# Other units for the value projections, late value chunks, and side blocks of a fused differential attention and gated layer

## The reference, cut to what matters

```
xn = layernorm(x)
q1, k1, q2, k2 (each 16 heads x 8), v (16 heads x 16) = split(xn @ Wqkv)
A_b = causal softmax(q_b k_b^T / sqrt(8)) @ v          for b = 1, 2
d = A1 - lam * A2;  d = d / rms(d) * (1 - LAMBDA_INIT)
ffn = (gelu(xn @ Wg0) * (xn @ Wg1)) @ Wlinear           in fp8
out = x + d @ Wproj + ffn
```

## Time and profile before

| | |
|---|---|
| median of three executions | 184.43 us |
| the profiled execution | 184.12 us |
| its span | 182.3 us |
| PE busy | 175.5 us, 96% |
| ACT busy | 163.2 us, 90% |
| DVE busy | 92.4 us, 51% |
| POOL busy | 63.5 us, 35% |
| exponentials (L497) | 97 instructions, 138.1 us |
| products with values (L1062) | 776 instructions, 78.1 us |
| scores (L1050) | 384 instructions, 48.3 us |

### The profile page before, as it was taken

The page is one execution under the profiler, slowest core; times in us unless marked ns, Lnnn a source line. Parts: engine busy times, 40 slices in busy tenths (PEclk is TensorE's granted clock), DMA queues, the critical chain, the costliest instruction groups (busy, mean ns, idle before and its releaser), DMA issues.

```text
span 182.3 us, 4305 instructions
## 1 busy us (share of the span) xinstructions
PE 175.5 (96%) x1816; PEld 76.3 (42%) x1816; DVE 92.4 (51%) x219; ACT 163.2 (90%) x146; POOL 63.5 (35%) x81
## 2 busy tenths in 40 slices
PE   6999999999999999999999999999999999989992
PEld 6785344543332333343234434334524434432481
DVE  1878789312233230640374121706542789979982
ACT  3586678999999999999999999999999999999820
POOL 8449920052017322360622063217303560323000
PEclk9999999999999999999999999999999999999999
DMA  5996888780000000000277875000000000000015
GB/s 152 382 333 227 219 197 201 175 189 19 0 0 5 0 0 4 0 4 0 42 204 179 210 173 127 0 0 4 4 0 0 4 0 4 0 0 4 0 58 180
DMA packets 8935, 15.02 MB, mean 82 GB/s; under 512 B 2000, under 2 KB 5584, under 8 KB 8912
## 3 DMA queue, kind: packets, MB, share of 16 engines
q1 hardware_dynamic: 8080, 13.92, 28.0%
q10 hardware_dynamic: 832, 0.79, 1.3%
HBM read 5.26 MB, written 1.05 MB: 35 GB/s over the span
## 4 chain that ended last, share of the span: by engine, by line
PE 82%; DVE 11%; ACT 2%; DMA 2%; issue 1%; DVEq 0%
PE ps L1062 35%; PE ps L1050 20%; PE ps L904 12%; PE ps L970 7%; PE ps L1098 4%; DVE o_t L719 2%; PE ps L914 2%; DMA x_sb<-L_attn_x 2%; DVE parts L625 1%; PE ps L894 1%; PE ps L1103 1%; DVE parts L737 1%; ACT L455 1%; DVE area L630 1%; DVE xn_t L763 1%
## 5 line engine op out<-in xcount | busy, mean ns | idle before, releaser
L497 ACT ACTIVATE probs<-ps,shift 128x1536 f32<-128x1536 f32 (+1 forms) x97 | 138.1, 1582 | 0.2 <-PE ps L1050 0.2
L1062 PE MATMUL ps<-probs,v_all 128*32 128x512 f32 (+3 forms) x776 | 78.1, 492 | 1.0 <-DVE o_t L719 0.8
L393 POOL TENSOR_SCALAR_AFFINE_SELECT probs<-probs 128x1024 f32<-128x1024 f32 (+1 forms) x40 | 36.7, 918 | 94.9 <-ACT probs L497 94.8
L1050 PE MATMUL ps<-q_st,k_st 32*128 32x512 f32 (+3 forms) x384 | 48.3, 411 | 0.0
L1050 PEld LDWEIGHTS ps<-q_st,k_st 32*128 32x128 f32 x384 | 22.5, 182 | 61.5 <-ACT probs L497 43.4
L719 DVE STREAM_TRANSPOSE o_t<-ps 128x512 f32<-128x512 f32 x16 | 11.5, 717 | 45.0 <-PE ps L1062 45.0
L1062 PEld LDWEIGHTS ps<-probs,v_all 128*32 128x32 f32 x776 | 16.4, 108 | 18.7 <-issue 9.7
L970 PE MATMUL ps<-area 128*128 128x512 fp8e4 x64 | 14.4, 379 | 0.2 <-DVE parts L625 0.2
L473 ACT ACTIVATE probs<-ps 128x512 bf16<-128x512 f32 x16 | 9.6, 597 | 3.7 <-PE ps L970 3.1
L644 DVE TENSOR_TENSOR area<-ps,probs 128x512 fp8e4<-128x512 f32 x16 | 10.9, 685 | 1.9 <-ACT probs L473 1.7
L970 PEld LDWEIGHTS ps<-area 128*128 128x128 fp8e4 x64 | 6.0, 98 | 8.0 <-issue 0.8
(11 more groups left out here) (90 smaller groups left out, 126.5 us busy)
## 6 DMA issues: line engine op xcount, KB each, us to landing
q_st<-parts SPq DMA_DIRECT2D x32, 128.0 KB, 2.8
k_st<-parts SPq DMA_DIRECT2D x32, 128.0 KB, 2.8
probs<-L_ffn_w_gating SPq DMA_DIRECT2D x4, 512.0 KB, 7.6
probs<-L_ffn_w_linear SPq DMA_DIRECT2D x1, 1024.0 KB, 12.4
out<-probs SPq DMA_DIRECT2D x3, 256.0 KB, 2.3
x_sb<-L_attn_x ACTq DMA_DIRECT2D x2, 256.0 KB, 5.1
w_q<-L_attn_Wqkv SPq DMA_DIRECT2D x1, 512.0 KB, 9.4
w_q<-L_attn_Wqkv SPq DMA_DIRECT2D x1, 256.0 KB, 4.2
```

Source lines behind the costliest of these rows:

```text
L393: pool.affine_select(out=blocks, in_=blocks, pattern=pattern, compare_op=ALU.is_ge, fill=0.0, base=0, channel_multiplier=-1).then_inc(mask ...
L497: act.activation(probs[:, at:at + PER_UNIT, cols], ps[:, 3 * (n % 2):3 * (n % 2) + 3, cols], ACT.Exp, bias=shift[:, br, 1, hg * BR + br:hg ...
L1050: ins = pe.matmul(ps[:, bank, at:at + wide * P], k_st[rows, g % STACKS, kb * P:(kb + 1) * P], q_st[rows, g % STACKS, queries], start=True, ...
L1062: ins = pe.matmul(ps[32 * j:32 * j + 32, 6, q0 % HALF:q0 % HALF + wide * P], v_all[:, g % HG, kb, 32 * j:32 * j + 32], probs[:, slot + j, ...
```

## The change

Value blocks 2 to 6 are projected one unit later (from unit 0 on one block a unit), and block 7 in two halves in units 8 and 9. Value chunks 3 to 8 of groups 0 to 3 are multiplied six units behind their scores in place of five, those of group 4 six behind for chunks 3 to 5 and five behind for 6 to 8 (before: five, and four); group 5 keeps its four behind for chunks 3 to 5 and its three for the last ones. The queries and keys of branch 2 stand in units 10 to 38 in place of 8 to 37. The blocks of the gated layer's last product, two squares, the residual additions, the first residual rows and the first output projection move. On DVE the copy of the last value block goes behind the first take, `keep(2, 0)` ahead of `split(6)`, and the `down` calls later. In the ending, residual 6 goes to the front.

```
-V_AT = {0: (1, 2), 1: (3,), 2: (4,), 3: (5,), 4: (6,), 5: (7,)}
-QK_AT = {8: (4, 0, 0, 256), 9: (4, 0, 256, 256), 13: (4, 1, 0, 512), 17: (5, 0, 0, 512), 20: (5, 1, 0, 256),
-         21: (5, 1, 256, 256), 25: (6, 0, 0, 512), 29: (6, 1, 0, 512), 32: (7, 0, 0, 256), 33: (7, 0, 256, 256),
-         37: (7, 1, 0, 512)}
+V_AT = {0: (1,), 1: (2,), 2: (3,), 3: (4,), 4: (5,), 5: (6,)}
+LAST_V_AT = (8, 9)
+QK_AT = {10: (4, 0, 0, 512), 14: (4, 1, 0, 512), 20: (5, 0, 0, 256), 21: (5, 0, 256, 256), 22: (5, 1, 0, 512),
+         26: (6, 0, 0, 512), 32: (6, 1, 0, 256), 33: (6, 1, 256, 256), 34: (7, 0, 0, 512), 38: (7, 1, 0, 512)}
 NORM_AT = 41
-DOWN_AT = {44: (0, 0, 4), 45: (0, 4, 8), 49: (1, 0, 8), 53: (2, 0, 8), 56: (3, 0, 4), 57: (3, 4, 8), 64: (4, 0, 8),
-           67: (5, 0, 4), 68: (5, 4, 8), 75: (6, 0, 8), 78: (7, 0, 4), 79: (7, 4, 8)}
-REST_AT, Y_AT = 83, 87
+DOWN_AT = {45: (0, 0, 4), 46: (0, 4, 8), 50: (1, 0, 8), 56: (2, 0, 4), 57: (2, 4, 8), 58: (3, 0, 8), 67: (4, 0, 4),
+           68: (4, 4, 8), 75: (5, 0, 8), 78: (6, 0, 4), 79: (6, 4, 8), 83: (7, 0, 8)}
+REST_AT, Y_AT = 87, (90, 91)
...
 def due(g, c):
-    late = ((5, 5), (5, 5), (5, 5), (5, 5), (5, 4), (4, 3), (3, 3), (3, 2))[g][c >= 6]
+    late = ((5, 6, 6), (5, 6, 6), (5, 6, 6), (5, 6, 6), (5, 6, 5), (4, 4, 3), (3, 3, 3), (3, 3, 2))[g][c // 3]
...
-                    if (g, c) in ((1, 2), (1, 5), (2, 5), (3, 0)):
+                    if (g, c) in ((1, 2), (2, 0), (2, 5), (3, 0)):
-                    if (g, c) in ((4, 4), (5, 2), (6, 0), (6, 5)):
+                    if (g, c) in ((4, 5), (5, 4), (6, 5), (7, 2)):
...
-            for b in range(0, TB, 2):
+            for b in range(0, TB - 2, 2):
                 values_in(b)
+            values_in(TB - 2, (0,))
...
-            keep(0, 0)
+            take(0, 0)
+            values_in(TB - 2, (1,))
+            divide(0, 0)
...
+            keep(2, 0)
             split(6)
-            keep(2, 0)
             split(7)
             keep(2, 1)
...
+                keep(3, 1)
                 down(0)
-                keep(3, 1)
...
+                if n in LAST_V_AT:
+                    if n == LAST_V_AT[0]:
+                        pe.wait_ge(v_out, TB - 1)
+                    project_values(TB - 1, LAST_V_AT.index(n))
...
+                elif g == 0 and c == 5:
+                    pe.wait_ge(v_out, TB)
...
-                    if n == Y_AT:
+                    if n in Y_AT:
                         pe.wait_ge(wp_in, 16 * 8)
                         pe.wait_ge(out_t_ready, 2)
-                        project(0, 0)
-                        project(1, 0)
+                        project(Y_AT.index(n), 0)
...
             def ending():
                 values_due(UNITS, 0, GROUPS)
                 values_due(UNITS + 1, 0, GROUPS)
+                pe.wait_ge(res_ready, TB // 2)
+                residual(6, start=True)
                 pe.wait_ge(out_t_ready, 3)
...
-                project(6, 0, start=True)
-                pe.wait_ge(res_ready, TB // 2)
-                residual(6)
+                project(6, 0)
```

More of the change, by code:

```diff
@@ L403, in _ @@
                     mask(g, c)
-                    if (g, c) in ((1, 2), (1, 5), (2, 5), (3, 0)):
-                        square_of(4 + ((1, 2), (1, 5), (2, 5), (3, 0)).index((g, c)))
-                    if (g, c) in ((4, 4), (5, 2), (6, 0), (6, 5)):
-                        residual(((4, 4), (5, 2), (6, 0), (6, 5)).index((g, c)))
+                    if (g, c) in ((1, 2), (2, 0), (2, 5), (3, 0)):
+                        square_of(4 + ((1, 2), (2, 0), (2, 5), (3, 0)).index((g, c)))
+                    if (g, c) in ((4, 5), (5, 4), (6, 5), (7, 2)):
+                        residual(((4, 5), (5, 4), (6, 5), (7, 2)).index((g, c)))
         @block.scalar
@@ L770, in turn_back, with values_in @@
                               ).then_inc(out_t_ready, 1)
-            def values_in(b):
-                dve.wait_ge(v_ready, b // 2 + 1)
-                for e in range(2):
+            def values_in(b, blocks=(0, 1)):
+                dve.wait_ge(v_ready, b // 2 + 1 + (b == TB - 2 and blocks == (1,)))
+                for e in blocks:
                     dve.tensor_copy(v_all[:, :, b + e, :].rearrange("p g (j w) -> p g j w", j=J)[:, :, :, 0:DV],
@@ L830, in _ @@
             with dve.If(large2 == 0):
+                keep(3, 1)
                 down(0)
-                keep(3, 1)
             all_of, first, last = slice(0, 32), slice(0, 16), slice(16, 32)
             take(4, 0)
-            down(1)
             own.step(difference(0, 0))
@@ L839, in _ @@
             take(4, 1)
+            down(1)
             own.step(difference(0, 1))
@@ L842, in _ @@
             take(5, 0)
-            down(2)
             own.step(difference(1, 0))
@@ L846, in _ @@
             take(5, 1)
+            down(2)
             differ(1, 1)
@@ L850, in _ @@
             mean_of(1, 1)
-            down(3)
             inverse_root(slice(0, 64))
@@ L858, in _ @@
             mean_of(2, 0)
+            down(3)
             take(6, 1)
@@ L916, in queries_keys, with project_values @@
                                  skip_group_check=True)
-            def project_values(b):
+            def project_values(b, only=None):
                 if b == 0:
                     pe.wait_ge(wv_in, 16)
-                for k in range(KC):
+                for k in range(KC) if only is None else (only,):
                     ins = by_quarters(V_BANK[b // 2], b % 2 * C, xn_t[:, k, b * P:(b + 1) * P], w_q[:, k, 2 * C:3 * C],
                                       k == 0, k == KC - 1)
-                if b % 2 == 1:
+                if (b % 2 == 1 or b == TB - 2) and only != 0:
                     ins.then_inc(v_ready, 1)
@@ L1092, in second_half @@
                 pe.wait_ge(o_taken, 2 * g + 1)
+                if g == 0:
+                    pe.wait_ge(v_out, kb + 1)
                 product(g, MIXED, first[1] * P, kb, wide, q0, True)
```

## The result

Seven executions of the changed kernel took 189.5 to 193.43 us, median 190.09; the kernel before beside them 184.31. The ratio is 1.029, interval 1.0276 to 1.0305. The forecast was 188.5 in a range of 187.1 to 189.4: the direction and most of the mechanism held, the range did not. In three of the seven (192.48 to 193.43) TensorE's clock was granted at half for some microseconds in the attention, in the other four (189.5 to 190.09) hardly or not at all, and the ratio is made of those four. The lowest of the four already lies over the range. In a second set of six it was 189.14 to 193.24. Both profiled executions of this kernel are among those with the lower clock.

The account below looks back on a forecast made before the run. PE and ACT, both near full, bound the kernel. ACT's losses of 5.7 less 1.46 before give +4.25; with +0.28 and -0.35, +4.2 on 184.12 is 188.3, by the median 188.5, range 187.1 to 189.4.

Parts of the forecast that it names:

- Bound by both engines, lost time adds up: Whole attention: PE 96% and ACT 90% busy; PE's waits are lost for ACT too, except for at most 0.7 us slack.
- Value block out of unit 0: Units 0 and 1: one block instead of two between scores 0 and 1; exponential 1 at 34.32, a gain of 0.32.
- Borders: Next group's first chunk waits for DVE's take: stall 0.47 at units 18, 30, 54 and 65, 0.15 at 42.
- Query block at 34: Unit 34: query block's first pass waits until DVE has emptied bank 7; stall 1.24, with scores 35 queued behind.
- Bound and collision at 45: Unit 45: v(3,2)'s second half waits behind branch 2's bound, stall 1.2 for 0.4; POOL's mask holding L567 adds 0.7.
- Rival A: Unit 45: the small L567 slips past POOL's mask, so time is 0.7 less, 187.8; chance 0.28.
- Units 90 and 91: Output projection's first pass moves into these half-empty units; their slack is gone and ACT loses 0.13 there.
- Ending: Residual 6 runs ahead of the wait for DVE on PE's last stretch: gain 0.35 (0 to 0.43).
- The +0.28 for the later last product: End of attention: ACT trails the last scores by 0.56 instead of 0.85, so the last product comes 0.28 later.
- Rival C: Four borders: waits shorter by half, 4 x 0.25 less; 187.5 with the collision, 187.0 without; chance 0.08.
- rival D: Late values cost PE 0.86 instead of 1.00 per unit, slack swallows every 0.47; 183.6 by the median; chance 0.02.
- rival B: More POOL collisions, at (7,2)'s mask and D7's cast: two more PE waits of 0.4 to 0.7, 189.4; chance 0.10.

Follow-up runs that it names:

- The last experiment: Changed kernel with the two halves of the first DOWN block back in units 44 and 45, filling part of PE's wait: median 189.24 us, ratio 1.0256.
- the kernel with the take first: Changed kernel with the take of v(3,2)'s first half ahead of the last part of branch 2's bound on DVE: median 188.67 us, ratio 1.0216.

## Why the prediction was right and wrong

ACT's losses, forecast and measured as the distance of the starts of its exponentials less 1.4227 us a unit. The last experiment stands for the changed kernel with the clock full, but for unit 55, where the kernel with the take first shows 0.15. The kernel before loses 1.45.

| units | forecast | clock full (part of the wait filled) | changed kernel, lower clock |
|---|---|---|---|
| 1 to 18 | 0 | 0.00 | 0.01 |
| 19 | 0.39 | 0.47 | 0.46 |
| 20 to 30 | 0.21 | 0.23 | 0.20 |
| 31 | 0.48 | 0.57 | 0.56 |
| 32 to 34 | 0.15 | 0.13 | 0.15 |
| 35 | 1.25 | 1.25 | 1.25 |
| 36 to 45 | 0.55 | 0.66 | 0.65 |
| 46 | 0.69 + 0.7 | 1.38 | 1.97 |
| 47 to 54 | 0 | 0.02 | 2.04 |
| 55 | 0.09 | 0.00 | 0.56 |
| 56 to 65 | 0.20 | 0.13 | 0.14 |
| 66 | 0.49 | 0.64 | 0.64 |
| 67 to 95 | 0.63 | 0.91 | 0.92 |
| sum | 5.83 | 6.38 | 9.57 |

*Bound by both engines, lost time adds up:* right. With the wait at unit 34, the one at 45 and the borders gone, 9.6 or 6.4 go back to 1.67.

*Value block out of unit 0:* right; exponential 1 is on ACT's own pace and units 1 to 18 lose nothing (0.59 before).

*Borders:* right in place and kind, small in size. At units 19, 31 and 66 ACT loses 0.47, 0.57 and 0.64 where 0.39, 0.48 and 0.49 were forecast. The next group's chunk starts 1.99 to 2.00 after the last one where 1.90 was reckoned. The prediction took the 0.77 from a take's start to PE from a half chunk's, and a half chunk's it is again in the changed kernel (101.23 to 102.00), but a whole chunk starts 0.86 after its take's start. At unit 65 it is 2.07, since the take too starts later behind its chunk (1.21 for 1.13). The four borders and unit 42 together: some 0.4.

*Query block at 34:* right to 0.01, shown by undoing it.

*Bound and collision at 45:* right, 1.38 for 1.39 in the kernel that stands in, the collision included; PE's wait was 1.73 for 1.9. Rival A is refuted: L568 took 0.93 to 0.94 in the four profiles in which it met the mask and ended with it, and 0.16 in all others. The Trainium skill, page "SBUF — State Buffer", section "Who interferes with whom", says that whichever of the two engines issues first has the shared pair of ports for the whole instruction, and the other is blocked until then. The trace agrees for this operation of 32 x 8. Not every TENSOR_SCALAR is held: in the kernel before, two of a single element ran inside a mask in 0.14 each, as long as outside one. Where the bound between them lies, no run shows:
```profile
95.22 0.64 POOL L393 TENSOR_SCALAR_AFFINE_SELECT probs<-probs 128x512 f32<-128x512 f32 x1 [3.20 <-ACT probs L497]
...
95.51 0.14 DVE L559 TENSOR_SCALAR norm_most<-norm_most 1x1 f32<-1x1 f32 x1
95.69 0.14 DVE L560 TENSOR_SCALAR flag<-norm_most 1x1 int32<-1x1 f32 x1
```

*Units 90 and 91:* wrong size. The forecast gave 0.13 to both and they lose 0.41. It counted the slack there as gone and nothing more, that is, it let the projection fit beside the half chunk as a half block does. In the kernel before four projections in a row take 1.06 to the next scores (157.89 to 158.95), so two would be 0.53, and a half chunk ahead of a half block takes 0.46. Together they take 1.20, some 0.2 more. That the change of form between neighbours (128 x 32 products, then 128 x 128 projections) is the reason was not tested.

*Ending:* of the 0.35 PE's part was 0.2, and no gain in time can be told with the ending alone (0.9997). The +0.28 for the later last product was right: from the start of the last half exponential to PE's end are 8.53 in the kernel before, 8.30 with the ending alone and 8.55 with the wait filled. What is left, 0.2 there, lies behind PE's end, in the output's issue.

*The sum:* with the clock full, 184.12 + (6.38 + 0.15 - 1.45) + 0.2 of ending is 189.4, where the forecast had 188.3 on the same base; the executions with hardly any fall took 189.1 to 190.1. So of the 1.6 us between forecast and median, about 1.1 is terms sized too small: some 0.4 at the borders, 0.3 at units 90 and 91, 0.3 in the ending, and 0.1 that the forecast had taken off its own sum. These terms alone put the time at the upper edge of the range, and all four executions at full or nearly full clock, 189.5 to 190.09, lie over it, by 0.1 to 0.7 more, which stays open. The falls of the clock lift the median of the seven further, from 189.66, the middle of those four, to 190.09.

*The clock:* a term put at nothing without a reason. The prediction said of the wait at 45 that it costs what ACT loses by it, 1.9 us of idle PE, and asked nothing of TensorE's clock. In the two profiles the granted clock falls from the 2.4 to the 1.2 GHz level behind that wait and stays there 6.8 us, and ACT loses another 3.0 us (0.59 at unit 46 and 2.02 behind it, against the column beside it, and 0.41 at 55). It happens in part of the executions. Three runs show that the wait is the cause: with the take first, or with part of the wait filled, all executions lie within 0.4%, and a wait of that length put into the kernel before brings the falls there.

Rival C and rival D are refuted by the border steps; rival B by the absence of any new wait at units 87 to 91 for DVE: the 4.1 us of waits for takes are those of the borders and of unit 45. For units 88 and after, the collision of residual and difference is there (L738 takes 1.27 beside the residual at 168.95, and 0.42 at 173.70) but the take came in time. Two sums of the rivals were off: C without the collision is 188.5 - 1.0 - 0.7 = 186.8, not 187.0, and in D the 2.62 less 0.43 hold two and a half chunks, of 0.87 each, not three. Neither changes the outcome.

## What to carry to other kernels

When two engines are both full, price a moved block by what it stood between: a block of other work between the last product into a bank and the first into the same bank hides the whole copy-out, and its move costs the copy-out less what is left between. A wait of TensorE is not only its own length: in this kernel one of 1.7 to 1.8 us took the clock down for some microseconds in part of the executions, and with 0.5 us of real work inside it no fall came in five executions. Look at the spread of the executions before explaining a median.

## What the runs showed of the hardware

- The clock's fall depends on the execution, not only on the kernel: the same program took 189.14 and 193.24. With waits of 1.30 and below at that place it was not seen; with 1.73 and 1.81 it came in part of the executions. The runs don't tell what sets which ones.
- At the lower level scores took 0.80 instead of 0.50 and a chunk 1.94 instead of 1.06.
- The falls in three profiles lasted 6.8, 6.8 and 3.4 us and began 0.4 to 1.0 behind the end of the wait.
- A whole chunk started 0.14 after the end of the take it waited for, a half chunk 0.05. A chunk that had waited took the same 1.00 to the next scores as one in full flow.
- A half chunk followed by a projection of another form cost 0.2 more than the two apart.
- A TENSOR_SCALAR of 32 x 8 took 0.94 beside a mask on POOL and 0.16 without; of 1 x 1 it took 0.14 inside a mask.
- The issue of one output DMA on SyncE took between 0.4 and 1.5 us at the same place in the program, from one profile to another.
